# Row sums of squares and per-row scales on quarter-width matmuls, a third buffer for rotated rows, and a new order on VectorE around them

## The reference

```
y = y_intra + y_inter                                  # per head and token: 128 values
rms = sqrt(mean(square(y), axis=-1) + 1e-5)            # one number per head and token
y = y / rms * gnorm_w
gate = hidden_states @ Wg.T
y = y * (gate * sigmoid(gate))
out = y.reshape(B, L, H * D) @ Wo.T
```

## Time and profile before

| what | value |
|---|---|
| runs | 2247.51 us median of 3 (2245.24 to 2248.74) |
| profiled execution, span from first to last instruction | 2250.0 us |
| TensorE matmul / weight load, busy | 2100.6 us (93%) / 1630.9 us (72%) |
| VectorE, ScalarE, GpSimd, busy | 1834.7, 1402.0, 1040.2 us |
| DMA | 182.31 MB, 81 GB/s over the span |
| one loop step | 56.8 us (from 1443.01 to 1499.83) |

### The profile page before, as it was taken

One profiled execution on the slowest core, in us unless ns is written; L12 is line 12 of the kernel. 1 busy time (PEld: TensorE's weight loads), 2 busy tenths in 40 slices (PEclk: granted clock), 3 DMA queues, 4 the chain that ended last, 5 costly groups with the idle time before them and its releaser, 6 DMA issues.

```text
span 2250.0 us, 34037 instructions
## 1 busy us (share of the span) xinstructions
PE 2100.6 (93%) x9568; PEld 1630.9 (72%) x9568; DVE 1834.7 (82%) x3440; ACT 1402.0 (62%) x2732; POOL 1040.2 (46%) x828
## 2 busy tenths in 40 slices
PE   5899999999999999998999999999999999999993
PEld 3677777777777777776677777777777777767772
DVE  5888888888888888868888888888888888737886
ACT  5566666666666666653566666666666666626782
POOL 1344444445454544434364545454545454534661
PEclk8899999999999999999899999999999999979996
DMA  7212121212121212135121212121212121217668
GB/s 255 79 46 58 46 56 47 56 47 56 44 58 38 64 37 66 35 87 173 38 66 38 67 36 62 35 63 38 66 38 66 38 66 38 76 61 255 217 215 315
DMA packets 147547, 182.31 MB, mean 81 GB/s; under 512 B 12935, under 2 KB 89319, under 8 KB 147454
## 3 DMA queue, kind: packets, MB, share of 16 engines
q1 hardware_dynamic: 137310, 155.52, 24.3%
q0 software_dynamic: 8704, 25.21, 3.1%
q10 hardware_dynamic: 1440, 0.58, 0.1%
HBM read 152.90 MB, written 28.37 MB: 81 GB/s over the span
## 4 chain that ended last, share of the span: by engine, by line
PE 77%; DVE 6%; issue 6%; POOL 4%; ACT 3%; DMA 2%; SPq 1%; DVEq 0%; POOLq 0%; ACTq 0%
PE PJ L1242 11%; PE PJ L1244 10%; PE PJ L1243 10%; PE OU L1242 5%; PE OU L1244 5%; PE OU L1243 5%; PE TR L1392 5%; PE YE L1244 2%; PE YE L1243 2%; PE YE L1242 2%; PE SC L1242 2%; PE CS L1242 2%; PE YI L1242 2%; PE CS L1244 2%; PE CS L1243 2%
## 5 line engine op out<-in xcount | busy, mean ns | idle before, releaser
L457 POOL TENSOR_TENSOR zl<-yb,zh 128x512 fp32r<-128x512 f32 x122 | 162.9, 1335 | 318.9 <-ACT zh L972 318.8
L1242 PE MATMUL OU<-woh,zh 128*128 128x512 f32 x488 | 230.4, 472 | 17.7 <-POOL wol L708 10.2
L1765 DVE TENSOR_TENSOR t<-PJ,cosb 128x512 f32<-128x512 f32 x160 | 110.3, 689 | 156.6 <-PE PJ L1244 110.7
L1242 PE MATMUL PJ<-xnh,wqh 128*128 128x512 f32 x544 | 225.4, 414 | 7.9 <-DVE t L1767 7.4
L988 ACT ACTIVATE qh<-t 128x512 fp32r<-128x512 f32 x128 | 80.9, 632 | 218.6 <-DVE t L1770 218.6
L1243 PE MATMUL PJ<-xnl,wqh 128*128 128x512 f32 x544 | 213.9, 393 | 0.0
L1244 PE MATMUL PJ<-xnh,wql 128*128 128x512 f32 x544 | 213.6, 393 | 0.0
L1242 PE MATMUL PJ<-xnh,wgh 128*128 128x512 f32 x512 | 209.1, 408 | 2.9 <-POOL wgl L708 2.9
L1243 PE MATMUL PJ<-xnl,wgh 128*128 128x512 f32 x512 | 204.7, 400 | 0.0
L738 POOL TENSOR_TENSOR gm<-gbc,amask 128x512 f32<-128x512 f32 x128 | 166.9, 1304 | 81.6 <-DMA gbc<-decay_exponents 48.3
L1244 PE MATMUL PJ<-xnh,wgl 128*128 128x512 f32 x512 | 204.4, 399 | 0.0
(11 more groups left out here) (547 smaller groups left out, 6381.7 us busy)
## 6 DMA issues: line engine op xcount, KB each, us to landing
gbc<-decay_exponents SPq DMA_DIRECT2D x128, 256.0 KB, 4.9
stage<-in_wq SPq DMA_DIRECT2D x72, 256.0 KB
stage<-in_wg SPq DMA_DIRECT2D x64, 256.0 KB
stage<-in_wo SPq DMA_DIRECT2D x64, 256.0 KB
gbc<-in_wm SPq DMA_DIRECT2D x48, 256.0 KB
stage<-in_wkv SPq DMA_DIRECT2D x34, 256.0 KB
experts<-in_wm SPq DMA_DIRECT2D x16, 512.0 KB, 5.9
experts<-expert_rows SPq DMA_DIRECT2D x16, 512.0 KB, 13.9
```

The lines of the kernel that those rows point to most:

```text
L457: nc.gpsimd.tensor_tensor(lo[:], yb[:, c, :], hi[:].bitcast(F32), ALU.subtract).then_inc(S["zlo"], 1)
L1242: nc.tensor.matmul(out_, a_hi, b_hi, start=first, stop=False)
```

## The change

- `squares(c)` and the four copies to `rs` go. `ACT.Square` writes straight to `rs[:, c, :]`. In the step after, behind `project(0)`, `sum_squares` makes four fp32 matmuls with 32 columns of ones each; chunk c lands on partitions 32c to 32c + 31 of TR. The program gives them the array's quarters of 128 rows by 32 columns.
- `rms_batch` reads TR and works on 128x512 in place of 128x2048, and writes to `zh`'s place.
- `spread_scales` makes four fp32 matmuls behind the value transposes: row c of the quarter is picked by a matrix with a one in its first row (`pick`) and spread on all 128 partitions, into the banks OU, YE, YI and SC. They get quarters of 32 rows by 128 columns. `late_z` reads these banks.
- `rope_at`: the third row (second query) goes to `y2` in place of `t2`. `rope(2)` waits for `tr` 1, `rope(3)` for `ropelo` 1 and `tr` 2, `rope(4)` for `ropelo` 2 in place of 3.
- On VectorE all four `late_z` stand between `rope(1)` and `rope(4)`; behind `rope(4)` come the turned keys' low part, the last query's low part, and only then `vw_lo(0)`.
- In `first_ups` the sums stand between the two products of the first `shared_up`, the scales behind it, ahead of `shared_up(half, 1)`.
- `onesr` goes; the biases' matmuls read `ones` under another type. `pick` costs five small memsets at the start.

```diff
             def rms_batch(at, half):
-                at.before("ssqc", 4)
-                a.activation(rs[:], rs[:], ACT.Ln, scale=1.0 / D, bias=rmseps[:, 0:1]).then_inc(S["rsln"], 1)
+                at.before("oproj", 4)
+                at.wait("ssq", 1)
+                a.activation(zhf[:], TR[:], ACT.Ln, scale=1.0 / D, bias=rmseps[:, 0:1]).then_inc(S["rsln"], 1)
                 at.wait("rsln", 1)
-                a.activation(rs[:], rs[:], ACT.Exp, scale=-0.5).then_inc(S["rms"], 1)
+                a.activation(zhf[:], zhf[:], ACT.Exp, scale=-0.5).then_inc(S["rms"], 1)
...
+            def sum_squares(at):
+                at.before("ysq", 4)
+                for c in range(NCH):
+                    ins = nc.tensor.matmul(TR[c * SUMS:(c + 1) * SUMS, :], ones[:, 0:SUMS], rs[:, c, :], start=True,
+                                           stop=True)
+                ins.then_inc(S["ssq"], 1)
+
+            def spread_scales(at):
+                at.wait("rms", 1)
+                at.before("accd", 4)
+                at.before("yt", 3)
+                at.before("y", 4)
+                at.before("wsc", 4)
+                for c in range(NCH):
+                    cs = slice(c * SUMS, (c + 1) * SUMS)
+                    ins = nc.tensor.matmul(TOU[c][:], pick[cs, :], zhf[cs, :], start=True, stop=True)
+                ins.then_inc(S["spread"], 1)
...
-                        def squares(c):
-                            at.wait("ysq", c + 1)
-                            if c:
-                                at.wait("ssqc", c)
-                            nc.tensor.matmul(TR[:], ones[:], y2[:], start=True, stop=True).then_inc(S["ssq"], 1)
...
                                 at.before("q3lo", 1)
+                            elif i == 2:
+                                at.wait("tr", 1)
+                            elif i == 3:
+                                at.wait("ropelo", 1)
+                                at.wait("tr", 2)
                             else:
-                                at.wait("ropelo", i - 1)
-                            if i == 2:
-                                at.wait("tr", 2)
+                                at.wait("ropelo", 2)
```

More of the change, by code:

```diff
@@ L46 @@
 XQ = 6
-CONSTS = 17
+CONSTS = 19
+SUMS = P // NCH
 CONST_DMAS = 10
@@ L1115, in step @@
                                 exp_g(c + 1)
-                            if c:
-                                at.wait("ssq", c)
-                                if c == 1 and first and half == 0:
+                            if first and half == 0 and c < 2:
+                                if c == 1:
                                     act.wait_ge(cf_out, 32)
-                                a.activation(rs[:, c - 1, :], TR[:], ACT.Copy).then_inc(S["ssqc"], 1)
-                            at.wait("y", c + 1)
-                            a.activation(y2[:], yb[:, c, :], ACT.Square).then_inc(S["ysq"], 1)
-                        at.wait("ssq", 4)
-                        a.activation(rs[:, 3, :], TR[:], ACT.Copy).then_inc(S["ssqc"], 1)
+                                    square(0)
+                                    square(1)
+                            else:
+                                square(c)
             def attention(half):
@@ L1349, in scores @@
                                 at.before("wsc", 4)
+                                if not first:
+                                    at.wait("z", 4)
                             else:
@@ L1399, in step @@
                             turn_logits(3)
+                        if not first:
+                            sum_squares(at)
                         at.before("gated", 4)
@@ L1409, in step @@
                         at.wait("vraw", 1)
-                        at.before("ssqc", 4)
+                        if not first:
+                            at.wait("rsln", 1)
                         for i in range(4):
@@ L1415, in step @@
                             turn_decays(0)
+                        if not first:
+                            spread_scales(at)
                         proj_q(1)
@@ L1486, in flush, with shared_up @@
                     out_proj(at, c, hi=TZ[c][0], lo=TZ[c][1], bank=TOU[c])
-            def shared_up(half, f):
+            def shared_up(half, f, products=(0, 1)):
                 blk, j = f // 2, f % 2
                 rows = slice(blk * L, (blk + 1) * L)
-                for i, bank in enumerate(UP[f % 2]):
+                for i in products:
+                    bank = UP[f % 2][i]
                     for k in range(KC):
@@ L1495, in shared_up @@
                                   k == KC - 1)
-                ins.then_inc(u_up, 1)
+                if products[-1] == 1:
+                    ins.then_inc(u_up, 1)
             def first_ups(half):
@@ L1501, in first_ups @@
                 at.before("gated", 4)
-                shared_up(half, 0)
+                shared_up(half, 0, (0,))
+                sum_squares(at)
+                shared_up(half, 0, (1,))
                 pe.wait_ge(wsplit_lo, shared_base(half) + 4 + 2)
-                at.before("ssqc", 4)
+                spread_scales(at)
+                at.wait("rsln", 1)
                 at.before("stt", 3)
@@ L1527, in shared_down @@
                     product(t, 1)
-                    nc.tensor.matmul(DN[half][t][:], onesr[0:2, :], b3s, start=False, stop=True).then_inc(u_down, 1)
+                    nc.tensor.matmul(DN[half][t][:], ones[0:2, :].bitcast(F32R), b3s, start=False, stop=True).then_inc(u_down, 1)
             attention(0)
@@ L1570, in expert_up @@
                         False)
-                nc.tensor.matmul(bank, onesr[0:2, :], mb12[i % 4], start=False, stop=True).then_inc(m_up, 1)
+                nc.tensor.matmul(bank, ones[0:2, :].bitcast(F32R), mb12[i % 4], start=False, stop=True).then_inc(m_up, 1)
             def turn_h(i):
@@ L1584, in expert_down @@
                 mm3(MO[i % 2][:], mhh[i % 4], mhl[i % 4], w3h[i % 2], w3l[i % 2], True, False)
-                nc.tensor.matmul(MO[i % 2][:], onesr[0:2, :], mb3[i % 4], start=False, stop=True).then_inc(
+                nc.tensor.matmul(MO[i % 2][:], ones[0:2, :].bitcast(F32R), mb3[i % 4], start=False, stop=True).then_inc(
                     m_dn, 1)
@@ L1830, in step @@
                                 late_z(at, 0)
+                                late_z(at, 1)
                             rope(2, 1)
+                            if not first:
+                                late_z(at, 2)
                             rope(3, 0)
+                            if not first:
+                                late_z(at, 3)
                             if first:
@@ L1843, in step @@
                                         knh[:].bitcast(F32), ALU.subtract).then_inc(S["knlo"], 1)
-                        if not first:
-                            late_z(at, 1)
+                        at.wait("ropehi", 5)
+                        v.tensor_tensor(ql[:, 3, :], rope_at[4], qh[:, 3, :].bitcast(F32),
+                                        ALU.subtract).then_inc(S["q3lo"], 1)
+                        vw_lo(0)
                         weigh(0)
@@ L1848, in step @@
                         for c in range(NCH):
-                            if 0 < c < 3 and not first:
-                                late_z(at, c + 1)
                             at.wait("whi", c + 1)
```

46 lines of the change are left out of this document (22 added, 24 removed).

## The result

The changed kernel takes **2273.4 us** (median of 4 runs, 2271.0 to 2282.2), the kernel before 2246.4 beside it: a ratio of 1.0135, 95% interval 1.0108 to 1.0163. It is slower by 1.4%, 27 us. The profiled execution, the longest of the four, has a span of 2280.1 against 2250.0. One execution of a later kernel, of twelve of the one that copies the scales, took 4432 us and is left out of its numbers.

The account below looks back on a forecast made before the run. TensorE was taken as the bound: 30 steps x (1.61 us added work - 1.70 stops regained) = -3, plus 5 behind the halves, is +2 on a 2250.0 profile; on the runs' median 2249 us, no change, range 2168 to 2300.

Parts of the forecast that it names:

- its own case: TensorE's narrow products in a group overlap in part, 2.59 us per group: 2249 us, range 2237 to 2262, chance 0.46.
- the case without overlap: Rival: TensorE's narrow products follow one another, groups up to 7.54 us per step, about 2323 us; chance 0.26.
- The groups: TensorE's narrow sums and scales: five slots of 0.43 plus extras, 2.59 us each, 5.18 per step replacing 3.57 of sums.
- The rival of full overlap: All four narrow products of a group stream at once on TensorE: groups 2.32 us per step, about 2172 us; chance 0.24.
- The change of division: Switching TensorE's array between full and narrow matmuls: 0.10 + 0.19 = 0.29 us per group.
- Stops covered: TensorE's stops at scores(0), out_proj and proj_q(0), mean 1.86 us per step, vanish all but 0.15: gain 1.7.
- VectorE's +0.24: VectorE's work and waits ahead of scores(0): moved instructions added, others and GpSimd's wait removed, net +0.24 us.
- chunk_state(0): Next late point on TensorE, needing vw_lo(0), 1.05 us; three score matmuls, 0.69, stand between; a stop over 0.5 means wrong.
- The half clock: Behind the stop at a half's end, 1.2 GHz from 991.9 to 994.6: already paid today, it only moves.
- Behind the halves: Scales ahead of shared_up(half, 1) wait for ScalarE's Ln and Exp: +2.4 us behind each half, 2 x 2.4 = +5.
- the late scales of the third rival: ScalarE reaches Ln late, spread_scales stops TensorE in the loop: each us above the 1.7 cover costs 30, 2279; chance 0.04.

Follow-up runs that it names:

- the one that copies the scales: Changed kernel with ScalarE copying the scales from the four banks into SBUF and late_z at its old places: 2243.4 us, ratio 1.0015 to the kernel before.
- the run on one quarter: Kernel with scales copied into SBUF, all eight narrow products put on the same quarter of the array: 2391.7 us against 2243.4.
- The third place by itself: Kernel before the change with only the third buffer for turned rows and VectorE's order keys' low part, last query's low part, vw_lo(0): 2223.6 us, ratio 0.9913.
- filling the stops: Changed kernel plus ten unread matmuls per step, six ahead of scores(0)'s wait and four ahead of chunk_state(0)'s: 2262.4 us, ratio 1.0087 to the kernel before.

## Why the prediction was wrong, and its range right by luck

The forecast was no change, 2249, with 2237 to 2262 for its own case; measured were 2273, inside the whole range only because that reached up for the case without overlap. Neither that case nor the forecast is what happened, so that is luck. So is the step: 56.5 to 57.2 us were named, and a step without half clock takes 56.8, but as groups of 2.3 and stops of 2.9 us, where 5.18 and 0.15 were counted.

- **The groups.** "Chunk 1's first part then can start beside chunk 0's second, not beside its first" fell: all four start together. 5.18 us for both groups were 2.3, and a group from its start to the matmul behind it 1.0 to 1.1, where 2.4 to 2.8 was named as the sign of being right. The rival of full overlap had 2.32, and the run on one quarter shows both ends: 3.62 and 1.06 for the records of the sums. The change of division cost about the 0.29 taken from the earlier trace rows, whose lone matmul has 2 rows and not 32: 1.09 and 1.17 against 0.87 + 0.29. The Trainium skill ("TensorE: Matmul & The Clock Gate", section on packing small matmuls) gives 3.07 times for four quarters of 32 rows; by that a group was an estimated 1.13, and the trace agrees with 1.1.
- **Stops covered.** "TensorE reaches the same point 5.18 us later" is the step that failed most. The sums lie ahead of `proj_q(0)`, for which `rope(1)` waits (1.80 us in the step of 641.3): they delay VectorE as much as TensorE and cover nothing. Only the scales lie between, 1.2 us. VectorE's way from `rope(1)` to `ql` grew by nearly as much (next point), so the stop at `scores(0)` stayed, 1.76 for 1.65 with b = 0. The 1.86 us of stops that were to vanish became 2.9. The rival of full overlap had the same flaw with its 1.36 regained, so its 2172 missed by 101.
- **VectorE's +0.24** was +1.06 (from 16.10 to 17.16 us between `rope(1)` and `ql`). The sum moved instructions and left the others at their old times; with the new order the additions of `rope(2)` and `rope(4)` meet GpSimd at other points and took 1.74 for 1.14 and 1.15 for 0.89, which is 0.86 us. Behind `ql`, `vw_lo(0)` took 2.17 where 1.05 was counted. The third place by itself did what was said: `ql` waits for GpSimd no more, and alone it wins 21 us (2223.6 against 2244.7 beside it).
- **chunk_state(0)** "stops TensorE only if `scores(0)` was itself just waiting": the condition was right, and it came true in every step. The text named a stop over 0.5 us there as a sign of being wrong; it is 1.13 to 1.29.
- **The half clock** "only moves" was said of the halves' ends, and nothing was said of the loop. It is the rest of the loss in the first half: filling the stops took 15.7 us off 13 steps and with them the half clock.
- **Behind the halves** the scales stop TensorE for 3.9 us, and in the first half the last step and flush are 2.1 longer: +2.4 was near. Inside the loop the scales stop nothing; the late scales of the third rival did not come.
- **Left out**: the second half. There VectorE itself pauses behind the loop's turn, in the steps with b = 0. VectorE, then PE, of the changed kernel:

```profile
1288.34 0.72 DVE L1824 COPY hcoef<-coef 128x64 f32 x1 [0.46 <-issue]
1291.79 0.69 DVE L1797 TENSOR_TENSOR t<-PJ,cosb 128x512 f32<-128x512 f32 x1 [2.73 <-PE PJ L1251]
```

```profile
1291.39 0.40 PE L1251 MATMUL PJ<-xnh,wkvl 128*128 128x512 f32 x1
1293.94 0.50 PE L1249 MATMUL PJ<-xnh,wqh 128*128 128x512 f32 x1 [2.15 <-DVE t L1799]
```

The operand of 1291.79 was complete at 1287.8, and in the other five such steps `rope(0)` starts from 0.3 us ahead of to 1.2 us behind the end of `project(1)`, which the row names, so that is not the cause; VectorE did nothing from 1289.1 on. Before, VectorE ended its step 2.2 us ahead of `project(0)`, and 0.55 us showed at `proj_q(0)`; now it ends level with it, and 2.0 to 3.5 show in all six such steps of the 13. These stops add up to 14.1 us, 4.1 before: 10 of the second half's 31. When VectorE ends is not all of it: with the third place alone it still ends 2.2 us ahead, and 1.4 to 2.2 show. What the pause is, no run tested. Waiting for code is a guess, from its place at the loop's turn and from its absence in the first half.

## What to carry to other kernels

Before work is saved on the busiest engine, ask which events the next engine waits for: what lies ahead of the point where both meet again delays both and covers nothing. When an engine that had slack comes to the front, check what it meets: VectorE's instructions on two SBUF operands beside GpSimd's, row by row. And try the parts of a change alone: here one part won 0.9%, and the whole lost 1.4%.

## What the runs showed of the hardware

VectorE's instruction with two operands in SBUF, started inside one of GpSimd, took up to 1.80 us for 0.69, and a copy within SBUF 1.26 for 0.19; instructions with one operand in PSUM (products with cos and sin, 0.68 to 0.69; `late_z` from a bank, 0.74) never stretched. GpSimd's own instructions grew too, from 1.30 to 1.75. The Trainium skill ("SBUF — State Buffer", section "Who interferes with whom") says that a VectorE instruction with two SBUF inputs contends with a GpSimd instruction that reads SBUF, over a shared pair of ports that works as an exclusive lock; the trace agrees, with 1.74 us for an addition beside GpSimd and 0.69 without. Four fp32 products of two parts each overlap fully on four quarters, at 1.1 us the group; on one quarter they take 3.6.
